# Two graph attention layers: another order of the steady pair on all five engines, and one signal for each group of scores

## What is computed

```python
# layer 0                                       # layer 1, on the x that layer 0 leaves
q, k, v = x@Wq.T, x@Wk.T, x@Wv.T + bv           # q, k, v = x@Wq + bq, x@Wk + bk, x@Wv + bv
s = q.k * 384**-0.5 + (adj + adj)               # s = q.k / sqrt(32) + beta * adj
s = where(any(s != 0, row), s, -inf)            # s = where(adj > 0, s, -9e15)
o = nan_to_num(softmax(s)) @ v                  # o = softmax(s) @ v
x = layernorm(x + o@Wo.T + bo)                  # x = layernorm(x + o)
```

## Time and profile before

| | us |
|---|---|
| time, median of 3 runs (range) | 2106.66 (2102.52 to 2108.08) |
| the profiled execution, its own time | 2102.98 |
| its span, first to last instruction | 2101.1 |

### The profile page before, as it was taken

One profiled execution on the slowest core, in us unless ns is written; L12 is line 12 of the kernel. 1 busy time (PEld: TensorE's weight loads), 2 busy tenths in 40 slices (PEclk: granted clock), 3 DMA queues, 4 the chain that ended last, 5 costly groups with the idle time before them and its releaser, 6 DMA issues.

```text
span 2101.1 us, 85420 instructions
## 1 busy us (share of the span) xinstructions
PE 2033.8 (97%) x23808; PEld 1910.1 (91%) x23808; DVE 1813.3 (86%) x8324; ACT 1884.3 (90%) x7816; POOL 1644.0 (78%) x2187
## 2 busy tenths in 40 slices
PE   6899999999999999999999999999999999999984
PEld 5799989999999999999999999999999999999974
DVE  4688889988989989888889888889889889888885
ACT  4699989999999999999999999999999999999885
POOL 3677878888888888888888888888888888788874
PEclk9999999999999999999999999999999999999997
DMA  4345555555555555555555555555555555555554
GB/s 147 73 107 134 136 134 127 140 134 125 141 134 126 140 134 128 138 134 129 137 134 129 137 134 131 135 134 132 134 134 136 130 134 136 130 134 137 122 125 109
DMA packets 225441, 274.22 MB, mean 131 GB/s; under 512 B 25680, under 2 KB 225360, under 8 KB 225360
## 3 DMA queue, kind: packets, MB, share of 16 engines
q1 hardware_dynamic: 225360, 273.26, 54.2%
HBM read 46.67 MB, written 25.17 MB: 34 GB/s over the span
## 4 chain that ended last, share of the span: by engine, by line
POOL 56%; issue 27%; PE 5%; POOLq 3%; DVE 3%; DMA 3%; SPq 2%; ACT 1%; DVEq 0%; ACTq 0%
POOL prob L1515 12%; POOL flip L1488 10%; POOL norm L1449 6%; POOL x_late L1500 5%; POOL y L1507 4%; POOL x_bo L1465 4%; POOL adj L1478 4%; POOL mask L1476 3%; POOL flip L1491 3%; POOL norm L1446 2%; DMA prob0T<-flip 2%; SPq L292 2%; POOL norm L1453 1%; PE r_bank L408 1%; PE r_bank L409 1%
## 5 line engine op out<-in xcount | busy, mean ns | idle before, releaser
L807 ACT ACTIVATE prob<-neg_s,heads 128x128 f32<-128x128 f32 x3072 | 1190.7, 393 | 17.7 <-DVE flip L1141 7.9
L807 ACT ACTIVATION_READ_ACCUMULATOR prob<-neg_s,heads 128x1 f32 x3072 | 591.6, 193 | 0.0
L1515 POOL TENSOR_TENSOR prob<-prob,heads 128x512 f32<-128x512 f32 x384 | 389.2, 1042 | 92.4 <-DVE heads L1213 92.4
L408 PE MATMUL r_bank<-xT_hi,w_hi 128*128 128x256 f32 x1152 | 356.4, 309 | 16.0 <-DVE xT_lo L1147 9.7
L1488 POOL TENSOR_TENSOR flip<-neg_s 128x768 f32<-128x768 f32 x128 | 236.0, 1843 | 169.1 <-DMA prob0T<-flip 161.5
L1125 DVE CUSTOM_DVE_ANT_0 neg_s<-s_bank,bias 128x128 f32<-128x128 f32 x1536 | 333.5, 286 | 18.9 <-PE s_bank L458 12.1
L1125 DVE CUSTOM_DVE_ANT_0 neg_s<-s_bank,adj 128x128 f32<-128x128 f32 x1536 | 333.5, 285 | 6.8 <-PE s_bank L458 6.7
L408 PE MATMUL r_bank<-x1T_hi,w_hi 128*128 128x256 f32 x1152 | 330.3, 287 | 3.5 <-DVE x1T_lo L1147 1.6
L410 PE MATMUL r_bank<-xT_hi,w_lo 128*128 128x256 f32 x1152 | 327.0, 284 | 0.0
L409 PE MATMUL r_bank<-xT_lo,w_hi 128*128 128x256 f32 x1152 | 326.8, 284 | 0.0
L409 PE MATMUL r_bank<-x1T_lo,w_hi 128*128 128x256 f32 x1152 | 324.2, 281 | 0.0
(11 more groups left out here) (85 smaller groups left out, 5472.2 us busy)
## 6 DMA issues: line engine op xcount, KB each, us to landing
prob0T<-flip SPq DMA_DIRECT2D x512, 192.0 KB, 3.6
prob1T<-stage SPq DMA_DIRECT2D x512, 192.0 KB, 3.6
x_in<-in_x_dram SPq DMA_DIRECT2D x128, 192.0 KB, 3.3
out_dram<-y SPq DMA_DIRECT2D x128, 192.0 KB, 2.7
adj<-in_adj_dram SPq DMA_DIRECT2D x256, 64.0 KB, 2.7
prob<-in_L_gnn_Wq_dram SPq DMA_DIRECT2D x1, 576.0 KB, 4.5
...
```

The lines of the kernel that those rows point to most:

```text
L408: pe.matmul(dst, a_hi(c), b_hi(c), start=(c == 0), stop=False)
L807: act.activation(prob[layer][:, h, :], neg_s[layer][:, h, :], ACT.Exp, bias=neg_max[layer][:, h:h + 1], scale=-1.0, accum_out=row_sum[laye ...
L1515: pool.tensor_tensor(prob[0][:, hs, :], prob[0][:, hs, :], inv_sum0[:, hs].unsqueeze(2).to_broadcast([P, HC, N]), ALU.mult).then_inc(probn ...
```

## The change

Nothing that is computed changes, and no buffer, transfer or instruction form. Each of the five engines gets another order of `body`; `first` and `last` are written anew to lead into it and out of it; body 3 is peeled as well, so that 58 bodies run; `RING_USERS` follows TensorE's new order. `scores` raises `s_done` once, with its last matmul, and `negate` waits once for each group of 12 heads in place of four times (`qk_out`, which waits for an older count, is adjusted). The diff, without most of `first` and `last`:

How many pairs are peeled, and the order of users of the four accumulator banks:

```diff
-BODY_FROM = 3
+BODY_FROM = 4
...
-RING_USERS = ["g0_4", "v1_1", "v0_1", "x1t0", "g0_5", "x1t1", "xt0", "pv0_0",
-  "pv1_0", "xt1", "g1_0", "g1_1", "ot_0", "g0_0", "g1_2", "g1_3",
-  "g1_4", "wo_0", "pv1_1", "pv0_1", "g0_1", "g1_5", "g0_2", "g0_3",
-  "ot_1", "wo_1", "v0_0", "v1_0"]
+RING_USERS = ["g0_5", "x1t1", "v0_0", "pv1_0", "pv0_0", "ot_0", "g1_0", "g1_1",
+  "v1_0", "wo_0", "g1_2", "v0_1", "xt0", "g1_3", "xt1", "g1_4",
+  "pv1_1", "pv0_1", "ot_1", "g0_0", "g0_1", "g0_2", "g0_3", "g1_5",
+  "wo_1", "v1_1", "x1t0", "g0_4"]
```

SyncE, the body:

```diff
 def body(r, off):
     n = Pair(r, off)
-    m5, m4, m3, m2, m1, p1, p2 = (n.plus(-5), n.plus(-4), n.plus(-3), n.plus(-2), n.plus(-1), n.plus(1), n.plus(2))
+    m5, m4, m3, m1, p1, p2 = (n.plus(-5), n.plus(-4), n.plus(-3), n.plus(-1), n.plus(1), n.plus(2))
     spread_probs(1, m4, 1)
+    spread_probs(0, m1, 1)
     load_adj0(p1)
-    spread_probs(0, m1, 1)
-    load_adj1(m2)
     store(m5, 1)
+    load_adj1(m1)
+    load_x(p2)
     spread_probs(1, m3, 0)
     spread_probs(0, n, 0)
-    load_x(p2)
     store(m4, 0)
```

TensorE, `scores`:

```diff
                            kT[layer][q.parity][rows, c, m], start=True, stop=True)
-            if c == C - 1:
-                mm.then_inc(s_done[layer], 1)
+        mm.then_inc(s_done[layer], 1)
```

TensorE, the body:

```diff
     m4, m3, m2, m1, p1 = (n.plus(-4), n.plus(-3), n.plus(-2), n.plus(-1), n.plus(1))
+    project_qk(1, m3, 5, r)
     project_out0(m2, 1, r)
+    project_v(1, m3, 1, r)
+    transpose_x1(m2, 0, r)
+    project_qk(0, n, 4, r)
+    project_qk(0, n, 5, r)
+    scores(1, m3, 0, r)
+    transpose_x1(m2, 1, r)
     project_v(0, n, 0, r)
-    project_v(1, m3, 0, r)
-    scores(1, m3, 0, r)
-    project_qk(0, n, 4, r)
-    project_v(1, m3, 1, r)
-    project_v(0, n, 1, r)
-    transpose_x1(m2, 0, r)
-    project_qk(0, n, 5, r)
-    transpose_x1(m2, 1, r)
-    transpose_x(p1, 0, r)
+    attend(1, m4, 0, r)
     attend(0, m1, 0, r)
-    attend(1, m4, 0, r)
     scores(0, n, 0, r)
-    transpose_x(p1, 1, r)
+    transpose_out1(m4, 0, r)
     project_qk(1, m2, 0, r)
     project_qk(1, m2, 1, r)
-    transpose_out1(m4, 0, r)
-    project_qk(0, p1, 0, r)
+    project_v(1, m2, 0, r)
+    project_out0(m1, 0, r)
     project_qk(1, m2, 2, r)
+    project_v(0, n, 1, r)
+    transpose_x(p1, 0, r)
     project_qk(1, m2, 3, r)
+    scores(1, m3, 1, r)
+    transpose_x(p1, 1, r)
     project_qk(1, m2, 4, r)
-    project_out0(m1, 0, r)
-    scores(1, m3, 1, r)
     attend(1, m4, 1, r)
     attend(0, m1, 1, r)
+    scores(0, n, 1, r)
+    transpose_out1(m4, 1, r)
+    project_qk(0, p1, 0, r)
     project_qk(0, p1, 1, r)
-    project_qk(1, m2, 5, r)
-    scores(0, n, 1, r)
     project_qk(0, p1, 2, r)
     project_qk(0, p1, 3, r)
-    transpose_out1(m4, 1, r)
```

ScalarE, `qk_out`:

```diff
-        act.wait_ge(s_done[layer], q.plus(-2).count(HC, 1, HC))
+        act.wait_ge(s_done[layer], q.plus(-2).count(1, 1, 1))
```

ScalarE, the body:

```diff
 def body(r, off):
     n = Pair(r, off)
-    m5, m4, m3, m2, m1, p1, p2 = (n.plus(-5), n.plus(-4), n.plus(-3), n.plus(-2), n.plus(-1), n.plus(1), n.plus(2))
-    out1T_out(m4, 0)
-    exps(1, m3, 0, 2, 4)
+    m5, m4, m3, m2, m1, p1 = (n.plus(-5), n.plus(-4), n.plus(-3), n.plus(-2), n.plus(-1), n.plus(1))
+    high_o0T(m1, 0)
+    exps(0, m1, 1, 10, 12)
+    exps(1, m3, 0, 0, 10)
+    qk_out(1, m2, 0, r)
+    exps(1, m3, 0, 10, 12)
+    qk_out(1, m2, 1, r)
+    values_out1(m2, 0)
+    norm_apply1(m5, 1)
+    exps(0, n, 0, 0, 4)
+    qk_out(1, m2, 2, r)
+    high_xT(p1, 0)
+    exps(0, n, 0, 4, 6)
     high_xT(p1, 1)
-    qk_out(1, m2, 0, r)
-    exps(1, m3, 0, 4, 6)
-    qk_out(1, m2, 1, r)
-    exps(1, m3, 0, 6, 8)
+    qk_out(1, m2, 3, r)
+    exps(0, n, 0, 6, 8)
+    qk_out(1, m2, 4, r)
+    out1T_out(m4, 1)
+    exps(1, m3, 1, 0, 2)
+    high_o0T(m1, 1)
+    exps(0, n, 0, 8, 12)
     qk_out(0, p1, 0, r)
-    exps(1, m3, 0, 8, 10)
-    exps(0, n, 0, 0, 2)
-    exps(1, m3, 0, 10, 12)
-    qk_out(1, m2, 2, r)
-    exps(0, n, 0, 2, 8)
-    qk_out(1, m2, 3, r)
-    norm_apply1(m5, 1)
-    qk_out(1, m2, 4, r)
-    exps(0, n, 0, 8, 10)
-    exps(1, m3, 1, 0, 2)
-    exps(0, n, 0, 10, 12)
-    high_o0T(m1, 1)
-    out1T_out(m4, 1)
-    qk_out(1, m2, 5, r)
+    exps(1, m3, 1, 2, 8)
     qk_out(0, p1, 1, r)
-    exps(1, m3, 1, 2, 6)
     qk_out(0, p1, 2, r)
     qk_out(0, p1, 3, r)
-    exps(1, m3, 1, 6, 12)
-    norm_apply1(m4, 0)
+    exps(1, m3, 1, 8, 12)
+    norm_apply0(m1, 0)
+    qk_out(1, m2, 5, r)
     exps(0, n, 1, 0, 4)
-    norm_apply0(m1, 0)
-    exps(0, n, 1, 4, 6)
-    values_out1(m2, 0)
-    qk_out(0, p1, 4, r)
-    exps(0, n, 1, 6, 8)
-    norm_apply0(m1, 1)
-    exps(0, n, 1, 8, 12)
     values_out1(m2, 1)
     high_x1T(m1, 0)
-    exps(1, m2, 0, 0, 2)
+    qk_out(0, p1, 4, r)
+    norm_apply0(m1, 1)
     qk_out(0, p1, 5, r)
+    exps(0, n, 1, 4, 6)
     high_x1T(m1, 1)
-    high_xT(p2, 0)
-    high_o0T(n, 0)
+    exps(0, n, 1, 6, 10)
+    norm_apply1(m4, 0)
+    out1T_out(m3, 0)
```

VectorE, `negate`:

```diff
-            dve.wait_ge(s_done[layer], q.count(HC, g, b + 1))
-            dve.sem_inc(dve_passed, 1)
+                dve.wait_ge(s_done[layer], q.count(1, g, 1))
+                dve.sem_inc(dve_passed, 1)
```

VectorE, the body:

```diff
 def body(r, off):
     n = Pair(r, off)
-    m5, m4, m3, m2, m1, p1, p2 = (n.plus(-5), n.plus(-4), n.plus(-3), n.plus(-2), n.plus(-1), n.plus(1), n.plus(2))
-    low_x1T(m2, 1)
+    m5, m4, m3, m2, m1, p1 = (n.plus(-5), n.plus(-4), n.plus(-3), n.plus(-2), n.plus(-1), n.plus(1))
+    norm_input1(m5, 1)
     low_o0T(m1, 0)
-    norm_input1(m5, 1)
-    low_xT(p1, 1)
-    flip_probs(0, m1, 1)
+    abs_max(m1, 1)
+    inverse_sums0(m1, 1)
     attention_out1(m4, 0)
     negate(0, n, 0, (0, 1, 2, 3))
-    norm_input1(m4, 0)
+    flip_probs(0, m1, 1)
+    add_residual0(m1, 0)
     inverse_sums1(m3, 0)
     flip_probs(1, m3, 0)
-    add_residual0(m1, 0)
+    values_out0(n, 1)
+    low_xT(p1, 0)
     negate(1, m3, 1, (0, 1, 2, 3))
+    low_xT(p1, 1)
+    norm_input0(m1, 0)
+    low_o0T(m1, 1)
+    attention_out1(m4, 1)
     abs_max(n, 0)
     inverse_sums0(n, 0)
-    low_o0T(m1, 1)
     negate(0, n, 1, (0, 1, 2, 3))
+    norm_input1(m4, 0)
     flip_probs(0, n, 0)
-    norm_input0(m1, 0)
     add_residual0(m1, 1)
     norm_input0(m1, 1)
-    attention_out1(m4, 1)
+    inverse_sums1(m3, 1)
     flip_probs(1, m3, 1)
-    inverse_sums1(m3, 1)
+    low_x1T(m1, 0)
+    negate(1, m2, 0, (0, 1, 2, 3))
+    low_x1T(m1, 1)
     values_out0(p1, 0)
-    negate(1, m2, 0, (0, 1, 2, 3))
-    values_out0(p1, 1)
-    low_x1T(m1, 0)
-    abs_max(n, 1)
-    inverse_sums0(n, 1)
-    low_xT(p2, 0)
```

GpSimd, the body, and the start of `first`:

```diff
 def body(r, off):
     n = Pair(r, off)
-    m5, m4, m3, m2, m1 = (n.plus(-5), n.plus(-4), n.plus(-3), n.plus(-2), n.plus(-1))
+    m5, m4, m3, m2, m1, p1 = (n.plus(-5), n.plus(-4), n.plus(-3), n.plus(-2), n.plus(-1), n.plus(1))
+    normalise0(m1, 1)
+    inverse_std(1, m5, 1)
+    residual1(m4, 0)
+    make_bias1(m2, 0)
+    make_bias1(m2, 1)
     late_x1(m3, 0)
-    make_bias1(m3, 1)
-    residual1(m4, 0)
-    inverse_std(1, m5, 1)
-    residual0(n, r)
     fold_scores0(n, 0)
+    late_x1(m3, 1)
+    normalise0(n, 0)
+    inverse_std(0, m1, 0)
+    residual1(m4, 1)
     inverse_std(1, m4, 0)
-    normalise0(n, 0)
-    late_x1(m3, 1)
-    make_bias1(m2, 0)
-    inverse_std(0, m1, 0)
     inverse_std(0, m1, 1)
-    residual1(m4, 1)
+    residual0(p1, r)
     fold_scores0(n, 1)
-    normalise0(n, 1)
...
 def first():
-    q0, q1, q2 = (Pair(0, k) for k in range(3))
+    q0, q1, q2, q3, q4 = (Pair(0, k) for k in range(5))
+    residual0(q0, 0)
+    make_bias1(q0, 0)
+    make_bias1(q0, 1)
+    residual0(q1, 0)
+    low_weights(WQ1)
     fold_scores0(q0, 0)
```

More of the change, by code:

```diff
@@ L577, in first @@
                 project_qk(0, q2, 4, 0)
+                project_qk(0, q2, 5, 0)
+                transpose_x1(q0, 0, 0)
+                transpose_x1(q0, 1, 0)
+                project_v(0, q2, 0, 0)
+                attend(0, q1, 0, 0)
+                project_qk(1, q0, 0, 0)
+                scores(0, q2, 0, 0)
+                project_qk(1, q0, 1, 0)
+                project_v(1, q0, 0, 0)
+                project_qk(1, q0, 2, 0)
+                project_out0(q1, 0, 0)
                 project_v(0, q2, 1, 0)
-                transpose_x1(q0, 0, 0)
@@ new lines, in first @@
+                scores(1, q0, 0, 0)
+                project_qk(0, q3, 5, 0)
+                project_v(0, q3, 0, 0)
+                transpose_x1(q1, 1, 0)
+                project_v(0, q3, 1, 0)
+                scores(0, q3, 0, 0)
+                attend(0, q2, 0, 0)
+                project_qk(1, q1, 0, 0)
+                project_qk(1, q1, 1, 0)
+                project_qk(1, q1, 2, 0)
+                project_out0(q2, 0, 0)
+                scores(1, q0, 1, 0)
+                project_v(1, q1, 0, 0)
@@ L620, in last @@
+                transpose_out1(z5, 0, LOOP_N)
+                project_v(0, z1, 1, LOOP_N)
                 project_qk(1, z3, 2, LOOP_N)
+                transpose_x(z0, 0, LOOP_N)
                 project_out0(z2, 0, LOOP_N)
+                scores(1, z4, 1, LOOP_N)
+                attend(1, z5, 1, LOOP_N)
```

(39 more changed lines are left out.)

619 lines of the change are left out of this document (330 added, 289 removed).

## The result

| | before | after |
|---|---|---|
| time, median of 8 runs each (range), us | 2106.74 (2102.52 to 2108.09) | 2113.52 (2109.69 to 2117.25) |
| ratio, 95% interval | | 1.0032 (1.0023 to 1.0041) |
| profiled execution / its span, us | 2102.98 / 2101.1 | 2113.25 / 2111.4 |
| steady body, mean of 50 in that execution, us | 31.446 | 31.451 |

The changed kernel is slower by 6.8 us, just beyond the bound of 0.3%, where 2101.5 (2090 to 2115) was forecast. Counting every PE group at its price, the changed kernel is 4.9 us behind at 150 us, 5.4 at 1970, and 10.3 at the end: the fill, then nothing in the loop, then the drain. In which stretch that execution of before is 3.8 us better than its median, the trace does not say, so the size of the two parts is only rough.

What follows compares the result with a forecast made beforehand. PE's own sequence, 31.43 us per body without waits, was taken as the bound; 58 bodies x 0.09 = 5.2 us off 2102.98 gives 2097.8, and the median 3.7 higher makes 2101.5, range 2090 to 2115.

Steps and rivals of the forecast that it cites:

- PE's floor: PE's steady body without waits, counted from each group's neighbours: 31.29 us, a net 0.14 saved.
- The place of the wait: PE waits at `attend(0, m1, 1)` for the DMA into `prob0T`, 0.05 us in every body.
- The one signal with the last matmul instead of the first bank's costs nothing ... I take the lower end: Between `scores` on PE and `negate` on DVE: later signalling costs nothing, at most 0.22 us; start of `negate` taken as 1.13.
- the reads of banks: Three DVE reads, `low_x1T(m2, 1)`, `values_out0(n, 0)` and `low_o0T(m1, 0)`: 0.44 us each, 0.24 more if at full duration.
- the statistics: `norm_input1(m5, 1)` on DVE, ahead of `abs_max(m1, 1)`: 0.88 us.
- the leg through POOL and the DMAs: From the start of `normalise0`: POOL's product, the flip, four DMAs and their landing, 11.11 us without slack.
- the chain: From `scores(1, m3, 0)` over DVE, POOL and DMAs to `attend(0, m1, 1)`: 18.26 to 18.72 us, where PE needs 18.21.
- The slower rival: `attend(0, m1, 1)` waits for the flip's DMAs by more than the 0.14 saved; at 18.55 us, 2118 us; chance 0.21.
- the steady gain: Saving in the steady bodies: 31.34 instead of 31.43 us each, 58 x 0.09 = 5.2 us.
- First and last bodies ... I take 0: Peeled bodies at start and end: no row prices them, estimated at 5.6 us either way, taken as 0.
- The rival that fill and drain eat the gain: The steady bodies do get faster, but start and end lose 5.6 us: about 2107 us; chance 0.10.
- The signals cost PE no time: On PE, nothing is appended to `scores`, 0.88 to its next group; the rival claimed 0.11 us each, 2095 us, chance 0.04.

Runs made afterwards that it cites:

- the mend: Changed kernel with first fold and normalise ahead of GpSimd's other work, second pair's x loaded first, first pair's values projected before the second pair's transpose: 2107.22 us.
- all three causes mended: Changed kernel with mended first part, wait for scores next to the first negate, and other loop-head slots for DVE (64) and POOL (110): 2101.89 us.
- POOL's start alone: Changed kernel with only GpSimd's order in the first part altered, first fold and `normalise0` ahead of its other steps: 2111.69 us.

## Why the prediction was wrong

**PE's floor was right.** 31.29 was counted from the neighbours of each group; with the wait at the attend gone, the body is 31.31. The prices of the earlier trace rows hold in another order.

**The place of the wait was right, its size was not.** The step that failed is "The one signal with the last matmul instead of the first bank's costs nothing ... I take the lower end". It costs 0.15 (1.28 against 1.13), inside the bounds of 0 to 0.22 but only in part for the reason given there: 0.05 is the later signal, 0.10 the wait that sits one sequencer instruction too early. The other terms of that body miss by +0.10 (the reads of banks), -0.08 (the statistics) and -0.13 (the leg through POOL and the DMAs), together -0.11; without the 0.15 the chain would have fitted. So the mean wait is 0.12 instead of 0.05 and the body 31.45, as before, instead of 31.34. With four signals the wait goes, the body is 31.32 and the time 7.8 less. With the wait next to the head the time falls by 6.8, but the profiled execution shows only a small part of it in the body; the way of the rest is not shown.

**The slower rival came near.** It decided from a chain of 18.35; by the mean wait the chain is 18.21 + 0.12 = 18.33. By itself it only takes the steady gain away. It does not make the kernel slower.

**"First and last bodies ... I take 0" failed, twice.** The bound of 5.6 us was about right for the fill (6.3 by the mend), but its sign and its place could have been worked out. `first` was in the diff: POOL's queue shows the steps put ahead of the first fold, and one of them needs a transfer. The walk through the order was made for the steady body only. The end has a cause that no row prices in advance: a pause behind the loop, moved onto the ring (4.0).

**The rival that fill and drain eat the gain** had half of the mechanism, with 2107 and a chance of 0.10. It held the ends, but not that the steady gain would be missing too. By the number alone the slower rival's 2118 is nearer, by luck: it put the loss into the bodies, which are no longer than before. With all three causes mended in the steady order as changed, the time is 2101.89, and 2101.5 was forecast. That nearness is partly luck: the body in that run is 31.43, not the 31.34 forecast, and the mended fill is better than the one before (PE's busy time in the first 100 us is 78.0 against 72.00).

**The signals cost PE no time**, as said: `scores` to its next group is 0.88 with one signal and with four. The four updates stand 0.04 apart, but show no tail on PE.

**What stays open.** With the fill mended alone, or POOL's start alone, the body is 31.51 to 31.52 instead of 31.45, with a longer wait at the attend. The DMA leg is 6.08 to 6.09 in these, and 6.10 to 6.12 in the two runs with the wait next to the head whose bodies are 31.42 and 31.43; it is 6.02 in the changed kernel. SyncE issues the four DMAs at the same times in all of them (the last 2.02 to 2.03 after the flip's end), but the last landing comes at 6.03 to 6.05 instead of 5.98. So the transfers themselves take longer, and no run tells why.
